# Moving half of the next pair's token transposes, and the work on them, ahead of the current pair's output products

## The chip, the cores and the metric

The kernel runs on one core of one Trainium2 chip. The metric is the device time of one execution in microseconds. TensorE multiplies matrices, VectorE and ScalarE do elementwise work, GpSimd small helper operations, and SyncE issues most DMAs. Each engine takes its own instructions in order; semaphores order them among each other.

## The reference

Input x has 8 chunks of 512 tokens of 512 features. In short:

```
xn = layernorm(x)
q, k, v = xn @ Wq.T + bq, xn @ Wk.T + bk, xn @ Wv.T + bv
context = phi(q) * cumsum(phi(k) * v, over tokens) * 32 ** -0.5     # phi(a) = elu(a) + 1
s = context @ Wo.T + bo
h = fwht(xn * SU_ug) ; up, gate = h @ W_up.T * .., h @ W_gate.T * ..   # 2048 hidden
z = fwht(silu(gate) * up * SU_dp) @ W_down.T * Wscale_dp
out = x + s * silu(z)
```

`fwht` is a Walsh-Hadamard transform, `phi(q)` and the cumulative sum are elementwise along the tokens. The kernel folds both transforms into the weights once.

## The kernel before

All matmuls are done on pairs of 16-bit parts: each operand is split into a high and a low half, and a product is three matmuls (high x high, high x low, low x high), of 128 x 128 by 128 x 512, accumulated in one PSUM bank. There are 8 banks of 128 x 512.

The eight chunks are worked in four pairs p = 0 to 3. Pair 0 also prepares the weights. In each of pairs 1 to 3, TensorE goes through 22 groups of seven products (a Strassen scheme: 7 products in place of 8, with sums of the tokens as operands), then through the "down" quads, four for each of the two chunks 2p and 2p+1 (`down_quad(c, a)`, 48 matmuls each), and after each chunk's quads through the output product of the attention (`out_product(c, t)`, four tiles t of 12 matmuls). Quads write the banks D_BANK = (7, 0, 1, 2), output products the banks R_BANK = (3, 4, 5, 6).

Between these stands the preparation of the next pair's tokens. The tokens x are loaded and normalised (`ln_stats`, `normalise_pair` on VectorE, the root on GpSimd). TensorE transposes them, in two halves kk = 0, 1, each 16 transposes of 128 x 128 (`transposes`), into the four banks R_BANK, the same that the output products use. Each half then goes through four steps:

- `x_high` (ScalarE): copies one bank aside (`b12`) and three as 16-bit high halves;
- `x_sums` (VectorE): seven operations of 128 x 512, sums for the scheme and low halves; the last one counts `x_read`;
- `t_high` (ScalarE): the high halves of the four sums, one operation of 128 x 2048;
- `t_low` (VectorE): their low halves, two operations of 128 x 1024; the last one counts `x_ready`.

The products of pair p+1 wait for `x_ready` of both halves.

On VectorE the order at the end of pair p is: the last additions of the products (`summed`), the maximum of the context, `ln_stats(p + 1)`, `normalise_pair(p + 1)` (counts `xn_ready`), the context's scale, eight `split_ctx`, `out_scale`, then `outputs(2p)`: for each tile the gate's argument from a D bank (`gate_argument`, counts `z_ready`), silu by ScalarE (`silu_outs`), the attention's part from an R bank (`gated`, counts `o_read`) and the residual. Then come `x_sums` and `t_low` of both halves, then `outputs(2p + 1)`. On TensorE the transposes of half 0 stand after quad 0 of chunk 2p+1, those of half 1 after its quad 2. `out_product(2p)` waits for the split context and its weights, and `out_product(2p + 1)` for `x_ready` of half 1. The diff shows the waits.

Lines to follow: transposes L1567, output product L1642, down quads L1608, products L1517; VectorE's normalisation L917, first context scale L857, splits L1049 and L1050, `out_scale` L1245, gate argument L1242, `gated` L1251, `x_sums` L942 to L951, `t_low` L960, additions L971; ScalarE's `x_high` L628 and L630, `t_high` L635. In pair 0, `first_transposes` is L1553, the first product group L1419, its token low halves L930, and a fold of weights L1452.

Of the kernel before, what the change touches and what calls it, by code (L numbers as in the profile page):

```python
# [26 lines left out]
PAIRS = CHUNKS // 2  # L27
# [82 lines left out]
def nth(p, g):  # L110

    return GROUPS * (p - 1) + g
# [42 lines left out]
def build(nc, x, wk_t, wv_t, wq_t, wo_t, ug_t, down_t, vecs, rows, ident_in, hada_in, out):  # L155
# [5 lines left out]
    with ExitStack() as ctx_stack:  # L161
# [98 lines left out]
        x_read, x_ready = sem("x_read"), sem("x_ready")  # L260
# [342 lines left out]
        def _(act):  # L603
# [13 lines left out]
            def x_high(p, kk):  # L617
                n = 2 * p + kk
                act.wait_ge(xp_done, 4 * n + 4)
                if not kk:  # L620
                    act.wait_ge(h_ready, 32 * p)
                    if p == 1:
                        act.wait_ge(plain_done, 4 * GROUPS)
                    else:
                        act.wait_ge(product_done, len(ORDER) * (p - 1))
                else:
                    act.wait_ge(t_made, 4 * (n - 2))
                act.activation(b12, bank[R_BANK[2]][:, :], ACT.Copy).then_inc(b12_copied, 1)  # L628
                for b, r in ((B11, 0), (B21, 1), (B22, 3)):
                    act.activation(xops[:, kk, HI, b, :], bank[R_BANK[r]][:, :], ACT.Copy).then_inc(x_hi, 1)  # L630

            def t_high(p, kk):
                n = 2 * p + kk
                act.wait_ge(t_made, 4 * (n - 2) + 4)
                act.activation(xops[:, kk, HI, T1:T4 + 1, :], t_sums, ACT.Copy).then_inc(x_hi, 1)  # L635
# [167 lines left out]
            def silu_outs(c):  # L803
                for t in range(TB):
                    act.wait_ge(z_ready, 4 * c + t + 1)
                    act.activation(gate_g[:, t % 2, :], gate_g[:, t % 2, :], ACT.Silu).then_inc(gate_ready, 1)  # L806
# [22 lines left out]
            for p in range(1, PAIRS):  # L829
                for g in range(GROUPS):  # L830
                    group(p, g)
                for j in (C22, C21, C12):
                    take(p, GROUPS - 1, j)
                silu_outs(2 * p)
                if p < PAIRS - 1:
                    x_high(p + 1, 0)
                    t_high(p + 1, 0)
                    x_high(p + 1, 1)
                    t_high(p + 1, 1)
                silu_outs(2 * p + 1)  # L840

        @block.vector
        def _(dve):
# [90 lines left out]
            def x_sums(p, kk):  # L934
                n = 2 * p + kk
                m = 4 * (n - 2)
                r = [bank[b][:, :] for b in R_BANK]
                dve.wait_ge(b12_copied, n - 1)
                dve.wait_ge(x_hi, 4 * n + 1)
                if kk:  # L940
                    dve.wait_ge(x_ready, n)
                dve.tensor_tensor(t_sums[:, 0, :], b12, r[0], ALU.subtract).then_inc(t_made, 1)  # L942
                dve.tensor_tensor(xops[:, kk, LO, B11, :], r[0], xops[:, kk, HI, B11, :], ALU.subtract)
                dve.wait_ge(x_hi, 4 * n + 3)
                dve.tensor_tensor(t_sums[:, 2, :], r[3], b12, ALU.subtract).then_inc(t_made, 1)
                dve.wait_ge(t_made, m + 1)
                dve.tensor_tensor(t_sums[:, 1, :], r[3], t_sums[:, 0, :], ALU.subtract).then_inc(t_made, 1)
                dve.tensor_tensor(xops[:, kk, LO, B21, :], r[1], xops[:, kk, HI, B21, :], ALU.subtract)
                dve.wait_ge(t_made, m + 3)
                dve.tensor_tensor(t_sums[:, 3, :], r[1], t_sums[:, 1, :], ALU.subtract).then_inc(t_made, 1)  # L950
                dve.tensor_tensor(xops[:, kk, LO, B22, :], r[3], xops[:, kk, HI, B22, :], ALU.subtract) \  # L951
                    .then_inc(x_read, 1)
# [92 lines left out]
            def split_ctx(p, n):  # L1045
                at = ctx_s(n)
                if n:
                    dve.wait_ge(ctx_split, 8 * p + n)
                prep.after(dve.tensor_scalar(at[:, HI, :], ctx_f(n), s_c[:, 0:1], None, ALU.mult))  # L1049
                dve.scalar_tensor_tensor(at[:, LO, :], ctx_f(n), s_c[:, 0:1], at[:, HI, :],  # L1050
                                         ALU.mult, ALU.subtract).then_inc(ctx_split, 1)
# [192 lines left out]
            def out_scale():  # L1244
                prep.after(dve.tensor_scalar(o_out[:, :], i_c[:, :], o_in[:, 0:1], None, ALU.mult))  # L1245
# [146 lines left out]
            for p in range(1, PAIRS):  # L1392
                for g in range(GROUPS):
                    group(p, g)
                last_sums(p)
                ctx_absmax(p)
                if p < PAIRS - 1:
                    ln_stats(p + 1)
                    normalise_pair(p + 1)
                ctx_scale(p)  # L1400
                for n in range(8):
                    split_ctx(p, n)
                out_scale()
                outputs(2 * p)
                if p < PAIRS - 1:
                    x_sums(p + 1, 0)
                    t_low(p + 1, 0)
                    x_sums(p + 1, 1)
                    t_low(p + 1, 1)
                outputs(2 * p + 1)  # L1410

        @block.tensor
        def _(pe):
# [142 lines left out]
                                mm.then_inc(xp_done, 1)  # L1556

            def transposes(p, kk):
                if kk:
                    pe.wait_ge(x_read, 2 * p - 1)  # L1560
                else:
                    pe.wait_ge(xn_ready, 8 * p + 8)
                for r, (c, k) in enumerate(((0, kk), (0, kk + 2), (1, kk), (1, kk + 2))):
                    if kk == 0:
                        pe.wait_ge(o_read, 8 * p - 8 + r + 1)
                    for t in range(TB):
                        mm = pe.transpose(bank[R_BANK[r]][:, t * P:(t + 1) * P],  # L1567
                                          x_ln[:, TB * c + t, k * P:(k + 1) * P], ident[:, :])
                    mm.then_inc(xp_done, 1)
# [44 lines left out]
            def down_quad(c, a):  # L1614
                for ts in ((0, 1), (2, 3)) if a == 0 else ((0, 1, 2, 3),):
                    down_part(c, a, ts)

            def out_product(c, t):
                p, cc = divmod(c, 2)
                n = GROUPS + (KB + 1) * cc + KB  # L1620
                slot = slot_of(p, n) if p else 0
                if t == 0:
                    pe.wait_ge(ctx_split, 8 * p + 8)
                    if p == 0:
                        pe.wait_ge(o_made, 1)
                    else:
                        pe.wait_ge(slot_loaded[slot], 16 * loads_into(p, n))
                    if p == 0 and cc == 0:
                        wait_taken(pe, 0, GROUPS - 1, PLAIN_BANKS.index(R_BANK[0]))
                        pe.wait_ge(stage_made, 4 * FP)  # L1630
                    elif cc == 0:
                        pe.wait_ge(summed, 3 * nth(p + 1, 0))
                    elif p < PAIRS - 1:
                        pe.wait_ge(x_ready, 2 * p + 4)
                if p == PAIRS - 1 and cc:
                    pe.wait_ge(o_read, 4 * c - 4 + t + 1)
                cols = slice(t * P, (t + 1) * P)
                n = 0
                for f in range(KB):
                    at = ctx_s(4 * (f % 2) + 2 * (f // 2) + cc)  # L1640
                    for s, ws in ((HI, HI), (HI, LO), (LO, HI)):
                        mm = pe.matmul(bank[R_BANK[t]][:, :], at[:, s, cols], o_weight(slot)[:, f, ws, :],  # L1642
                                       start=(n == 0), stop=(n == 3 * KB - 1))
                        n += 1
                mm.then_inc(o_done, 1)
# [3 lines left out]
            for p in range(PAIRS):  # L1649
                for g in range(GROUPS):  # L1650
                    if p == 0:
                        first_group(g)
                    else:
                        group(p, g)
                for a in range(KB):
                    if a or not p:
                        down_quad(2 * p, a)
                for t in range(TB):
                    out_product(2 * p, t)
                for a in range(KB):  # L1660
                    down_quad(2 * p + 1, a)
                    if a in (0, 2) and p < PAIRS - 1:
                        transposes(p + 1, a // 2)
                for t in range(TB):
                    out_product(2 * p + 1, t)

# [44 lines left out]
```

## Time and profile before

| | |
|---|---|
| median of 3 runs | 1337.85 us (1336.74 to 1338.49) |
| profiled execution, its own time | 1337.85 us |
| its span, first to last instruction | 1336.0 us |
| mean granted clock of TensorE | 0.998 of full speed |
| TensorE busy | 98% of the span |
| VectorE, ScalarE, GpSimd busy | 64%, 39%, 3% |

The profile's page gives busy times and the chain of work that ended last; the trace behind it gives every instruction with its start, its duration and what released it. Where a row has a bracket, this is the engine's idle time just before the row and what ended it. Rows without a bracket follow the one before without idle time worth naming. A matmul's record overlaps the next by up to 0.16 us, so differences of starts are used where pieces follow each other.

### The profile page before, as it was taken

To read this page: it belongs to the slowest core of one execution; us is meant where nothing else is said; L and a number is where in the kernel's file an instruction comes from. 1 tells how busy PE (TensorE), PEld (TensorE's weight loads), DVE (VectorE), ACT (ScalarE), POOL (GpSimd) and SP (SyncE) were. 2 spreads that over 40 slices of the span, in tenths; PEclk is the share of its full clock that TensorE was granted. 3 is DMA by queue.
4 is the path that set the end of the run, shared out by engine and by line. 5 is a ranking of instruction groups with operands and counts; after the bars stand their busy time and mean duration, and the time that the engine had idled before them with its cause. 6 is when DMAs were issued, how large, how long until landed. Compare 5 with 4: busy or idle time off the path is not lost.

```text
span 1336.0 us, 16024 instructions
## 1 busy us (share of the span) xinstructions
PE 1307.3 (98%) x6100; PEld 598.5 (45%) x6100; DVE 853.3 (64%) x1365; ACT 527.3 (39%) x815; POOL 41.8 (3%) x72
## 2 busy tenths in 40 slices
PE   5999999999999999999999999999999999999998
PEld 3434444444444444444454444444444444444443
DVE  6897999959446778655735765546735664555433
ACT  5844555540124655541014554442013654443000
POOL 0100100000000001000000000000000000000000
PEclk9999999999999999999999999999999999999999
DMA  9612555446255256435344233234344333333230
GB/s 370 249 75 106 188 200 205 176 179 218 81 214 185 97 201 222 158 127 187 107 148 157 99 123 126 97 124 170 114 157 135 132 112 126 105 117 116 105 126 32
DMA packets 47548, 199.38 MB, mean 149 GB/s; under 512 B 5104, under 2 KB 5360, under 8 KB 31984
## 3 DMA queue, kind: packets, MB, share of 16 engines
q1 hardware_dynamic: 41424, 176.87, 36.9%
q0 software_dynamic: 6048, 21.50, 4.3%
q8 instruction: 48, 0.79, 0.2%
q14 instruction: 28, 0.23, 0.1%
HBM read 153.26 MB, written 45.09 MB: 148 GB/s over the span
## 4 chain that ended last, share of the span: by engine, by line
PE 87%; DVE 5%; issue 3%; ACT 3%; DMA 2%; SPq 0%; DVEq 0%; ACTq 0%
PE bank L1517 37%; PE bank L1608 25%; PE bank L1419 15%; PE bank L1642 6%; PE bank L1452 2%; PE bank L1463 1%; ACT work L726 1%; DVE work L987 1%; ACT work L729 1%; PE bank L1567 1%; DVE work L977 1%; DVE work L971 1%; DMA h_all<-scr_f 1%; DMA work<-in_x 0%; DMA ring<-scr_d 0%
## 5 line engine op out<-in xcount | busy, mean ns | idle before, releaser
L1517 PE MATMUL bank<-xops,ring 128*128 128x512 f16 x2772 | 602.5, 379 | 3.9 <-DVE work L971 1.9
L1517 PEld LDWEIGHTS bank<-xops,ring 128*128 128x128 f16 x2772 | 269.6, 98 | 335.9 <-issue 7.0
L1608 PE MATMUL bank<-ring,h_all 128*128 128x512 f16 x1536 | 334.3, 379 | 0.2 <-DMA ring<-scr_d 0.2
L971 DVE TENSOR_TENSOR work<-bank,work 128x512 f32<-128x512 f32 x198 | 134.1, 686 | 181.9 <-PE bank L1517 167.9
L1419 PE MATMUL bank<-xops,ring 128*128 128x512 f16 x1056 | 238.5, 380 | 1.9 <-DVE xops L930 1.9
L1608 PEld LDWEIGHTS bank<-ring,h_all 128*128 128x128 f16 x1536 | 150.2, 98 | 180.4 <-DMA ring<-scr_d 0.7
L716 ACT ACTIVATE work<-bank 128x512 f32<-128x512 f32 x198 | 117.8, 595 | 245.1 <-PE bank L1517 245.1
L1419 PEld LDWEIGHTS bank<-xops,ring 128*128 128x128 f16 x1056 | 103.0, 98 | 142.0 <-issue 30.8
L806 ACT ACTIVATE gate_g<-gate_g 128x512 f32<-128x512 f32 x32 | 19.9, 630 | 229.5 <-DVE gate_g L1242 229.5
L746 ACT ACTIVATE h_all<-work 128x512 f16<-128x512 f32 x128 | 78.0, 624 | 73.3 <-DVE work L1010 73.2
L1019 DVE TENSOR_TENSOR h_all<-work,h_all 128x512 f16<-128x512 f32 x128 | 87.6, 686 | 8.0 <-ACT h_all L746 6.6
L1642 PE MATMUL bank<-ring,ctx 128*128 128x512 f16 x384 | 84.2, 379 | 0.0
L977 DVE SCALAR_TENSOR_TENSOR work<-work 128x512 f32<-128x512 f32 x64 | 44.2, 690 | 53.8 <-ACT work L729 53.6
L1242 DVE TENSOR_TENSOR gate_g<-bank,row 128x512 f32<-128x512 f32 x32 | 21.4, 689 | 69.7 <-PE bank L1608 69.1
L1010 DVE SCALAR_TENSOR_TENSOR work<-bank,up_out,work 128x512 f32<-128x512 f32 x56 | 41.8, 746 | 25.7 <-PE bank L1517 11.4
L1642 PEld LDWEIGHTS bank<-ring,ctx 128*128 128x128 f16 x384 | 37.6, 98 | 45.3
L739 ACT ACTIVATE work<-work,gate_out 128x512 f32<-128x512 f32 x72 | 51.1, 714 | 5.4 <-DVE work L971 5.0
L942 DVE TENSOR_TENSOR work<-work,bank 128x512 f32<-128x512 f32 x6 | 4.1, 688 | 75.6 <-ACT xops L630 75.6
L1010 DVE SCALAR_TENSOR_TENSOR work<-work,up_out 128x512 f32<-128x512 f32 x72 | 51.9, 744 | 0.3
L739 ACT ACTIVATE work<-bank,gate_out 128x512 f32<-128x512 f32 x56 | 38.0, 679 | 22.3 <-PE bank L1419 21.1
L992 DVE TENSOR_TENSOR_SCAN work<-work 128x512 f32<-128x512 f32 x32 | 39.2, 1224 | 1.1
L628 ACT ACTIVATE work<-bank 128x512 f32<-128x512 f32 x6 | 3.6, 597 | 90.2 <-PE bank L1567 90.2
(166 smaller groups left out, 877.9 us busy)
## 6 DMA issues: line engine op xcount, KB each, us to landing
ring<-scr_g SPq DMA_DIRECT2D x66, 1024.0 KB, 4.8
ring<-scr_d SPq DMA_DIRECT2D x32, 1024.0 KB, 4.8
scr_g<-ring SPq DMA_DIRECT2D x22, 512.0 KB, 3.3
h_all<-in_ug_t SPq DMA_DIRECT2D x8, 1024.0 KB, 14.4
x_res<-in_x SPq DMA_DIRECT2D x32, 256.0 KB, 3.4
out<-x_res SPq DMA_DIRECT2D x32, 256.0 KB, 6.8
scr_g<-ring POOLq DMA_DIRECT2D x14, 512.0 KB, 3.0
work<-in_x SPq DMA_DIRECT2D x6, 1024.0 KB, 6.5
```

Source lines behind the costliest of these rows:

```text
L716: act.activation(tile(g, j), chain_bank(g)[:, :], ACT.Copy).then_inc(copied, 1)
L739: act.activation(tile(g, j), src, ACT.Silu, scale=gate_out[:, at:at + 1]).then_inc(act_tiles, 1)
L746: act.activation(h[:, i, TILE_OF[j], HI, :], tile(g, j), ACT.Copy).then_inc(h_hi, 1)
L971: dve.tensor_tensor(tile(g, j), at[:, :], tile(g, j), ALU.add).then_inc(summed, 1)
L977: dve.scalar_tensor_tensor(tile(g, j), exp_tile(n), 1.0, tile(g, j), ALU.min, ALU.add) \
L992: dve.tensor_tensor_scan(tile(g, j), tile(g, j), tile(g, j), 0.0, ALU.add, ALU.bypass) \
L1010: dve.scalar_tensor_tensor(tile(g, j), src, up_out[:, at:at + 1], tile(g - 1, j), ALU.mult, ALU.mult).then_inc(h_made, 1)
L1019: dve.tensor_tensor(at[:, LO, :], tile(g, j), at[:, HI, :], ALU.subtract).then_inc(h_ready, 1)
L1419: mm = pe.matmul(plain_bank(g, j)[:, :], at[:, s, 2 * dh + kk, r, :], xops[:, kk, xs, PLAIN_B[dh][c], :], start=(n == 0), stop=(n == len(t ...
L1517: mm = pe.matmul(to[:, :], weight_of(slot, s, b, kk), xops[:, kk, xs, c, :], start=(a == 0 and m in (P1, P2, P5)), stop=(a == 5), skip_gro ...
L1608: mm = pe.matmul(bank[D_BANK[t]][:, :], at[:, s, cols], w[:, :, ws, :], start=(a == 0 and b == 0 and n == 0), stop=(a == KB - 1 and b == K ...
L1642: mm = pe.matmul(bank[R_BANK[t]][:, :], at[:, s, cols], o_weight(slot)[:, f, ws, :], start=(n == 0), stop=(n == 3 * KB - 1))
```

## The change

At the ends of pairs 1 and 2 half 0 of the next pair's tokens is taken earlier. TensorE issues its transposes between quads 2 and 3 of chunk 2p. VectorE does its `x_sums` and `t_low` before `out_scale` and `outputs(2p)`, and ScalarE its `x_high` and `t_high` before `silu_outs(2p)`. The transposes of half 1 move to after quad 0 of chunk 2p+1. The waits follow: half 0 waits for the last additions (`summed`) in place of `o_read`; half 1 waits for `o_read` of each tile and no longer for `x_read`; `out_product(2p)` waits for `x_ready` of half 0 (count 2p+3) in place of `summed`, and `out_product(2p + 1)` as before for that of half 1 (2p+4). At the end of pair 0 the order is as before, and in pair 3 there are no transposes.

```diff
--- before.py
+++ after.py
@@ -831,10 +831,11 @@
                     group(p, g)
                 for j in (C22, C21, C12):
                     take(p, GROUPS - 1, j)
-                silu_outs(2 * p)
                 if p < PAIRS - 1:
                     x_high(p + 1, 0)
                     t_high(p + 1, 0)
+                silu_outs(2 * p)
+                if p < PAIRS - 1:
                     x_high(p + 1, 1)
                     t_high(p + 1, 1)
                 silu_outs(2 * p + 1)
@@ -1400,11 +1401,12 @@
                 ctx_scale(p)
                 for n in range(8):
                     split_ctx(p, n)
+                if p < PAIRS - 1:
+                    x_sums(p + 1, 0)
+                    t_low(p + 1, 0)
                 out_scale()
                 outputs(2 * p)
                 if p < PAIRS - 1:
-                    x_sums(p + 1, 0)
-                    t_low(p + 1, 0)
                     x_sums(p + 1, 1)
                     t_low(p + 1, 1)
                 outputs(2 * p + 1)
@@ -1556,12 +1558,14 @@
                                 mm.then_inc(xp_done, 1)
 
             def transposes(p, kk):
-                if kk:
-                    pe.wait_ge(x_read, 2 * p - 1)
-                else:
+                if p == 1 and kk:
+                    pe.wait_ge(x_read, 1)
+                if kk == 0:
                     pe.wait_ge(xn_ready, 8 * p + 8)
+                    if p > 1:
+                        pe.wait_ge(summed, 3 * nth(p, 0))
                 for r, (c, k) in enumerate(((0, kk), (0, kk + 2), (1, kk), (1, kk + 2))):
-                    if kk == 0:
+                    if kk == (p > 1):
                         pe.wait_ge(o_read, 8 * p - 8 + r + 1)
                     for t in range(TB):
                         mm = pe.transpose(bank[R_BANK[r]][:, t * P:(t + 1) * P],
@@ -1628,10 +1632,12 @@
                     if p == 0 and cc == 0:
                         wait_taken(pe, 0, GROUPS - 1, PLAIN_BANKS.index(R_BANK[0]))
                         pe.wait_ge(stage_made, 4 * FP)
+                    elif p == 0:
+                        pe.wait_ge(x_ready, 4)
+                    elif p < PAIRS - 1:
+                        pe.wait_ge(x_ready, 2 * p + 3 + cc)
                     elif cc == 0:
-                        pe.wait_ge(summed, 3 * nth(p + 1, 0))
-                    elif p < PAIRS - 1:
-                        pe.wait_ge(x_ready, 2 * p + 4)
+                        pe.wait_ge(summed, 3 * nth(PAIRS, 0))
                 if p == PAIRS - 1 and cc:
                     pe.wait_ge(o_read, 4 * c - 4 + t + 1)
                 cols = slice(t * P, (t + 1) * P)
@@ -1655,12 +1661,16 @@
                 for a in range(KB):
                     if a or not p:
                         down_quad(2 * p, a)
+                    if a == 2 and 0 < p < PAIRS - 1:
+                        transposes(p + 1, 0)
                 for t in range(TB):
                     out_product(2 * p, t)
                 for a in range(KB):
                     down_quad(2 * p + 1, a)
-                    if a in (0, 2) and p < PAIRS - 1:
-                        transposes(p + 1, a // 2)
+                    if a == 0 and p < PAIRS - 1:
+                        transposes(p + 1, 1 if p else 0)
+                    if a == 2 and p == 0:
+                        transposes(1, 1)
                 for t in range(TB):
                     out_product(2 * p + 1, t)
```

## Rows read from the trace of the kernel before

**Rows 1.** The page's first part: busy us of each engine, share, instructions.
```profile
PE 1307.3 (98%) x6100; PEld 598.5 (45%) x6100; DVE 853.3 (64%) x1365; ACT 527.3 (39%) x815; POOL 41.8 (3%) x72
```

**Rows 2.** TensorE's waits: us in total, times, longest.
```profile
PE bank L1553 <- DVE work L917: 14.5, 1, 14.5
PE bank L1452 <- DVE h_all L1160: 2.5, 1, 2.5
PE bank L1517 <- DVE work L971: 1.9, 6, 0.3
```

**Rows 3.** TensorE in order of time: start us, us, engine, line, tiles.
```profile
615.00 36.42 PE L1608 MATMUL bank<-ring,h_all 128*128 128x512 f16 x168
651.26 10.52 PE L1642 MATMUL bank<-ring,ctx 128*128 128x512 f16 x48
...
671.98 1.91 PE L1567 MATMUL bank<-ident,work 128*128 128x128 f32 x16
673.72 20.88 PE L1608 MATMUL bank<-ring,h_all 128*128 128x512 f16 x96
694.44 1.91 PE L1567 MATMUL bank<-ident,work 128*128 128x128 f32 x16
...
730.25 10.65 PE L1517 MATMUL bank<-xops,ring 128*128 128x512 f16 x48 [0.23 <-ACT work L716]
...
959.99 10.52 PE L1642 MATMUL bank<-ring,ctx 128*128 128x512 f16 x48
```

**Rows 4.** VectorE in order of time, end of pair 1.
```profile
633.81 0.17 DVE L914 TENSOR_SCALAR rstd<-rstd 128x8 f32<-128x8 f32 x1 [4.14 <-POOL rstd L538]
634.02 3.74 DVE L917 TENSOR_SCALAR work<-work,mean_var,rstd 128x512 f32<-128x512 f32 x8
637.68 0.14 DVE L857 TENSOR_SCALAR pw<-ctx_max_all 128x1 f32<-128x1 f32 x1
...
648.78 0.21 DVE L1245 TENSOR_SCALAR o_out<-i_c,o_in 128x1 f32<-128x1 f32 x1
651.53 1.29 DVE L1242 TENSOR_TENSOR gate_g<-bank,row 128x512 f32<-128x512 f32 x2 [2.54 <-PE bank L1608]
...
662.07 0.74 DVE L1251 SCALAR_TENSOR_TENSOR s_f<-bank,o_out,row 128x512 f32<-128x512 f32 x1
```

**Rows 5.** VectorE in order of time, `x_sums` and `t_low` of half 0.
```profile
675.11 0.69 DVE L942 TENSOR_TENSOR work<-work,bank 128x512 f32<-128x512 f32 x1 [10.85 <-ACT xops L630]
...
680.84 2.36 DVE L960 TENSOR_TENSOR xops<-work,xops 128x1024 f16<-128x1024 f32 x2 [1.45 <-ACT xops L635]
```

**Rows 6.** ScalarE in order of time, the same half.
```profile
673.92 0.60 ACT L628 ACTIVATE work<-bank 128x512 f32<-128x512 f32 x1 [14.42 <-PE bank L1567]
...
678.82 1.91 ACT L635 ACTIVATE xops<-work 128x2048 f16<-128x2048 f32 x1 [2.84 <-DVE work L950]
```

**Rows 7.** VectorE in order of time, end of pair 2.
```profile
936.39 2.47 DVE L891 BATCH_NORM_STATS2 stats<-work 128x6 f32<-128x512 f32 x4 [1.55 <-DMA work<-in_x]
...
946.83 0.15 DVE L857 TENSOR_SCALAR pw<-ctx_max_all 128x1 f32<-128x1 f32 x1
...
957.92 0.21 DVE L1245 TENSOR_SCALAR o_out<-i_c,o_in 128x1 f32<-128x1 f32 x1
```

**Rows 8.** The chain that ended last, ahead of the first product.
```profile
19.87 2.40 DVE xops L930 x4
```

**Rows 9.** Stretches: length, busy us of each engine, TensorE's granted clock, DMA.
```profile
22.40:30.40 8.00, 8.00 (x46) 3.75 (x46) 5.21 (x16) 7.91 (x8) 0.70 (x2) 1.00 1.00 401
68.00:73.20 5.20, 2.78 (x13) 1.07 (x11) 5.17 (x6) 1.45 (x2) 0.00 (x0) 1.00 0.38 152
73.20:82.00 8.80, 8.74 (x29) 3.52 (x30) 8.05 (x28) 3.36 (x5) 0.68 (x2) 0.81 0.08 30
```

**Rows 10.** TensorE in order of time, the two early waits.
```profile
22.40 7.93 PE L1419 MATMUL bank<-xops,ring 128*128 128x512 f16 x36 [1.89 <-DVE xops L930]
...
73.26 1.51 PE L1452 MATMUL bank<-h_all,hada 128*128 128x512 f32 x2 [2.48 <-DVE h_all L1160]
```

## The prediction

> **What bounds the kernel now.** I read the page first. TensorE is busy 1307.3 of the 1336.0 us, the next engine (VectorE) 853.3 [rows 1]. So about 28.7 us of the span are all that any reordering could win, and every microsecond in which TensorE is made to wait is added to the time. The reader is to see there that nothing but TensorE's own stream sets the end.
>
> Next, who ends TensorE's waits [rows 2]. The largest are 14.5 us at the start and one of 2.5 at 70.8 us; the other seven lines have under 2 us each, the sums (L971) with six waits of up to 0.3 first among them. No line of the view names the transposes of the pair loop (L1567) or the output product (L1642). So the wait on `x_read` or on `o_read` before the transposes, and the wait on `x_ready` before the output product, which the change moves, cost nothing today.
>
> Then TensorE in order of time around the end of pair 1 [rows 3]. From 615.00 on each piece starts where the one before it ends, with no idle time named: 168 matmuls of down quads until 651.26 (3.5 quads in 36.26 us, so 10.36 each), there the output product of chunk 2 (as long as a quad, 48 matmuls), quad 0 of chunk 3, transposes from 671.98, two quads, transposes from 694.44, quad, output product, next pair. The first small wait comes only within the next pair's products, 0.23 us at 730.25; with four like it up to 783.86 they make 1.25 us.
>
> Last, VectorE and ScalarE over the same stretch [rows 4, 5, 6], because the change puts its work between the rows of these two. VectorE is the engine to look at: after the statistics of the layernorm it waits 4.14 us for GpSimd's root, then come eight normalisations, the scale of the context and its eight splits, back to back until 648.78. It idles only 2.5 us before the outputs of chunk 2, and then 10.85 us before `x_sums`.
>
> **The change part by part.** The first pair's boundary (pair 0 to 1) keeps its order: with p = 0 the transposes stand after quads 0 and 2 of chunk 1 as now, and the waits are the same numbers. The last pair has no transposes. What changes lies at the ends of pairs 1 and 2, so every term counts twice.
>
> *Work added or removed: none.* The 16 transposes of a half, 1.74 us (they start at 671.98 and the next quads at 673.72 [rows 3]), are issued once as before. The number of copies, sums and DMAs is the same. TensorE's busy time should stay.
>
> *Transposes of half 0, moved from after quad 0 of chunk 2p+1 to between quads 2 and 3 of chunk 2p.* The output product now starts at 651.26; quad 3 takes 10.36 before it; so quad 2 ends at 640.90. That is where the transposes go. They need `xn_ready`, the last normalisation: the eight L917 start at 634.02 and the next operation starts at 637.68 [rows 4], so they have 3.2 us to spare. In pair 2 the output product starts at 959.99 [rows 3], so quad 2 ends at 959.99 - 10.36 = 949.63 and the normalisations at 946.83 [rows 7]: 2.8 us to spare. Their wait on `summed` is for the pair's last addition, which stands ahead of all these on VectorE and so is long past. Cost: nothing now; it would cost what the loading of x is later than these 3 us. They no longer wait for `o_read`. Quad 3 then runs from 642.64 to 653.00, where the output product could start.
>
> *The new wait.* The output product of chunk 2p writes the banks that the transposes filled, so it must now wait until `x_sums` and `t_low` of half 0 have read them (`x_ready` 2p+3). How long does that take? Today, with VectorE free: transposes issued at 671.98, ScalarE's first copy at 673.92, `x_sums` from 675.11, ScalarE's wide copy 678.82 to 680.73, `t_low` from 680.84 to 683.20 [rows 5, 6]. From transposes to `x_ready` 11.22 us, of which VectorE's part, from its first subtraction, is 683.20 - 675.11 = 8.09 us.
>
> From 640.90 this would be done at 652.12, 0.9 us before the product: it would just fit, if VectorE were free at 644.03. It is not. VectorE works in order, and `x_sums` stands behind the eight splits of the context, which last until 648.78 (there `out_scale` starts today [rows 4]). So: 648.78 + 8.09 = 656.87, plus 0.13 from the end of the releasing VectorE group to the first matmul that it releases (a group of 2.40 us from 19.87, so 22.27 [rows 8], and 22.40 [rows 10]) = 657.00. TensorE could have started at 653.00. **Stall in pair 1: 4.00 us.**
>
> Pair 2 by the same rows: VectorE is free at 957.92 [rows 7], 0.4 us later in relation to TensorE because the second load of x landed later (1.55 us of idle at 936.39). 957.92 + 8.09 + 0.13 = 966.14 against 959.99 + 1.74 = 961.73. **Stall in pair 2: 4.41 us.** Together 8.41.
>
> The bounds of this term. Below: were ScalarE's copies done before, `x_sums` might run a little closer packed than 0.60 us each, but these rows already run back to back; I allow 0.3 us a pair. Above: the landing of x moves the end of the splits, by 0.4 us from one pair to the other; I allow 0.6 us a pair.
>
> *What is queued behind the wait.* On TensorE all the rest of the kernel. On VectorE, after `t_low`, come `out_scale` (0.21) and `outputs(2p)`. The quads of chunk 2p are by then done, so the first two gate arguments run at once, about 0.3 to 1.6 us after the output product's start. Today they run from 0.27 to 1.56 after it [rows 4]. So the output stage stands to the output product as today, its first tile waits 2.8 us for the product as today, and the banks that quad 0 of chunk 2p+1 wants are free as early. ScalarE's silus come after `t_high`, which is done 2.6 us before the product starts (5.62 us after `x_sums` begins [rows 5, 6]): no cost.
>
> *Transposes of half 1, moved from after quad 2 to after quad 0 of chunk 2p+1.* They wait for `o_read` of all four tiles. The last L1251 starts 10.8 us after the output product [rows 4] and the transposes 20.7 us after: 9 us to spare. Then 11.22 us to `x_ready`, against 1.74 + 31.08 (three quads) until the output product of chunk 2p+1 that now waits for it: 21 us to spare, where today there are 694.44 + 11.22 = 705.66 against 694.44 + 1.74 + 10.36 = 706.54, only 0.9. This slack is what the change gains, but it is slack at a place where TensorE did not wait. VectorE is idle there and the outputs of chunk 2p+1 stay as they are, so the next pair starts as now. DMAs are issued in the same order, each waits for TensorE or VectorE, and so moves along.
>
> *TensorE's clock.* A stall may cost more than its length. Where TensorE waited 2.48 us, until 73.26 [rows 10], the granted clock had been 1.00 and was 0.81 in the 8.8 us after it [rows 9]: of its two levels, 1.2 GHz for part of that stretch and 2.4 for the rest. That is 0.19 x 8.8 = 1.67 us lost. After the wait of 1.89 us before 22.40 the clock stayed 1.00 [rows 9, 10]. Ends: nothing (as after 1.89) and twice 1.67 (the stalls are 1.6 and 1.8 times as long as the one of 2.48). I take 1.67 each, because both stalls are nearer to, and longer than, the idle that lost it. Together 3.34.
>
> A page bears on this. The Trainium skill, "TensorE: Matmul & The Clock Gate", section "Why this matters for your kernels", advises to leave no idle gap of more than about 3 us between bursts of matmuls, since the clock falls back to half. Here the trace differs in size, since 2.48 us were enough; by the page as by the row both stalls would lose the clock, and with the clock kept, which the page would expect only of shorter stalls, the sum would be 3.34 us lower.
>
> **The sum.** The profiled execution took 1337.85 us for a span of 1336.0, so 1.85 lie outside it; it is also the median of the runs (1336.74 to 1338.49), so one sum serves for both. 1336.0 + 4.00 + 4.41 + 3.34 = 1347.75 of span, + 1.85 = **1349.6 us**, 0.9% slower.
>
> **The rivals.**
>
> 1. *The clock holds.* Stalls as worked out, no loss after them: 1337.85 + 8.41 = 1346.3; if one of the two loses it, 1347.9. For it: the gap of 1.89 us. Against: that of 2.48.
>
> 2. *The clock loses more.* Twice 1.67 after each stall: 1337.85 + 8.41 + 6.68 = 1352.9. For it: longer idle than any in the trace but the first; against: no row shows it.
>
> 3. *Not slower: the product does not wait.* This needs VectorE to be through `t_low` by 652.87, so `x_sums` to start by 644.8, 4.0 us before the splits end. That point decides. It could be only if the context were split or the normalisation done sooner, such as by GpSimd's root coming at once (VectorE waits 4.14 us for it in pair 1). Nothing in the change touches that chain. It would give 1337.9. If besides that the smoother boundary took away all the small waits of the next pairs, 2 x 1.25 us, 1335.3: even this is only 0.19%.
>
> 4. *The transposes wait as well.* If x lands over 3 us later, they stall TensorE before quad 3. But that wait mostly replaces the later one, as VectorE is late by the same amount: each further microsecond of lateness costs one, and no more. With 2 us in each pair 1353.6.
>
> **How the numbers follow.** Forecast (both or most of the clock loss) 0.70; the clock holds at one or both stalls 0.14; it loses more 0.07; transposes wait 0.02; no wait 0.05, of which nearly all is within the bound; something that makes it faster 0.02. I call 0.2% (2.7 us) about what a measurement of this kernel can tell from no change. Slower: 0.70 + 0.14 + 0.07 + 0.02 = 0.93; same 0.05; faster 0.02. The range: from the clock holding less 0.6 us for the packing and 0.4 for the run, 1345.3, to the clock losing twice, 1353.0. It leaves out "no wait" and the worst of rival 4.
>
> **What the profile after would show.** In the waits of TensorE a new line: the output product waiting for `t_low` on VectorE, twice, 4.0 and 4.4 us. In TensorE's timeline 16 transposes between quads 2 and 3 of chunks 2 and 4, with no idle before them. In VectorE's timeline `x_sums` directly behind the splits, with no idle before it, and no idle before the gate arguments. The granted clock at some 0.8 in the 9 us after each stall, and the output product taking some 12 us for 10.5. TensorE's busy time some 3.3 us higher by the slower clock alone. The second half's `x_ready` some 21 us ahead of its use. I am wrong if the context's splits end sooner in relation to TensorE, or if `x_sums` to `t_low` takes clearly less than 8.09 us.

## The result

The changed kernel took 1348.88 us (median of 4 runs, 1347.22 to 1349.52) against 1337.33 us for the kernel before in the same rounds (1336.74 to 1338.49). The ratio is 1.0084, with a 95% interval from 1.0065 to 1.0101: slower by 0.8%, or 11.55 us; 11.75 were forecast. The profiled execution took 1349.76 us, its span is 1347.9 us, 11.9 more than the span before. It is the longest of the changed kernel's five executions, so what its trace adds up to lies a little above the median.

First the waits of TensorE in the changed kernel (us in total, times, longest), which answer to [rows 2]:

```profile
PE bank L1555 <- DVE work L918: 14.6, 1, 14.6
PE bank L1648 <- DVE xops L961: 7.5, 2, 3.8
```

The second line is new. L1648 is the output product, L961 is `t_low`: twice the product waited for VectorE's last low half, 7.5 us together, and nothing like it stood in the kernel before.

TensorE in order of time at the ends of pair 1 and pair 2, against [rows 3]:

```profile
614.60 26.06 PE L1612 MATMUL bank<-ring,h_all 128*128 128x512 f16 x120
640.50 1.91 PE L1571 MATMUL bank<-ident,work 128*128 128x128 f32 x16
642.25 10.52 PE L1612 MATMUL bank<-ring,h_all 128*128 128x512 f16 x48
656.45 13.23 PE L1648 MATMUL bank<-ring,ctx 128*128 128x512 f16 x48 [3.68 <-DVE xops L961]
669.52 10.52 PE L1612 MATMUL bank<-ring,h_all 128*128 128x512 f16 x48
679.88 1.91 PE L1571 MATMUL bank<-ident,work 128*128 128x128 f32 x16
...
955.83 1.91 PE L1571 MATMUL bank<-ident,work 128*128 128x128 f32 x16
957.58 10.52 PE L1612 MATMUL bank<-ring,h_all 128*128 128x512 f16 x48
971.90 12.21 PE L1648 MATMUL bank<-ring,ctx 128*128 128x512 f16 x48 [3.79 <-DVE xops L961]
983.94 10.52 PE L1612 MATMUL bank<-ring,h_all 128*128 128x512 f16 x48
```

The transposes have no idle time before them, in either pair. The only gap is ahead of the output product. By starts it is 656.45 - (642.25 + 10.36) = 3.84 us in pair 1 (a quad takes 10.36 us by starts) and 971.90 - (957.58 + 10.36) = 3.96 in pair 2. Then the product itself is slow: from its start to the next quad's it is 669.52 - 656.45 = 13.07 us in pair 1 and 12.04 in pair 2, where 10.36 was usual. That is 2.71 and 1.68 us more for the same 48 matmuls.

So the sum is 3.84 + 3.96 of stall and 2.71 + 1.68 of slower product, 12.19. The changed kernel reached the half quad 0.40 us earlier (614.60, [rows 3] 615.00), which the change has no part in, and 0.1 is scattered: 11.9. This 0.40 is what is left of two larger differences that have nothing to do with the change. In the kernel before the clock was lost at 73.26 [rows 9, 10], in this execution it was not (1.00 there), and pair 1 began 1.9 us earlier; then TensorE waited 1.12 us at 505.17 and 0.43 at 523.89 for VectorE, of which the kernel before had 0.16. Single executions of one kernel differ by such amounts: the 27 of the kernel before below span 1335.57 to 1338.66 us.

VectorE over the same stretch, against [rows 4, 5]: the last split, then at once `x_sums`, `t_low`, `out_scale`, gate arguments.

```profile
633.25 0.17 DVE L915 TENSOR_SCALAR rstd<-rstd 128x8 f32<-128x8 f32 x1 [3.87 <-POOL rstd L538]
...
647.55 0.75 DVE L1051 SCALAR_TENSOR_TENSOR ctx<-ctx,s_c 128x512 f16<-128x512 f32 x1
648.22 0.68 DVE L943 TENSOR_TENSOR work<-work,bank 128x512 f32<-128x512 f32 x1
...
653.95 2.36 DVE L961 TENSOR_TENSOR xops<-work,xops 128x1024 f16<-128x1024 f32 x2 [1.45 <-ACT xops L635]
656.22 0.21 DVE L1246 TENSOR_SCALAR o_out<-i_c,o_in 128x1 f32<-128x1 f32 x1
656.47 1.29 DVE L1243 TENSOR_TENSOR gate_g<-bank,row 128x512 f32<-128x512 f32 x2
661.77 0.75 DVE L1252 SCALAR_TENSOR_TENSOR s_f<-bank,o_out,row 128x512 f32<-128x512 f32 x1 [4.01 <-PE bank L1648]
```

The reader sees the queue: the banks were filled at 642.3, but VectorE begins to read them at 648.22, when the eighth split is through, and ends at 656.31, 8.09 us later; 0.14 us after that the product starts.

And TensorE's granted clock (length, busy us and count, clock, DMA), in the gap and in the product of either pair:

```profile
652.70:656.40 3.70, 0.07 (x1) 0.83 0.65 230
656.40:669.50 13.10, 13.05 (x48) 0.79 0.04 17
968.00:971.80 3.80, 0.10 (x1) 1.00 0.65 231
971.80:983.90 12.10, 12.00 (x48) 0.86 0.03 14
```

The same view in short stretches shows when the clock changed:

```profile
655.20:655.40 0.20, 0.00 (x0) 0.50 0.97 410
662.00:662.50 0.50, 0.50 (x4) 1.00 0.00 0
972.00:972.30 0.30, 0.30 (x2) 1.00 0.53 219
972.60:973.00 0.40, 0.40 (x3) 0.50 0.00 0
976.00:976.50 0.50, 0.50 (x4) 1.00 0.00 0
```

In pair 1 the clock fell from 2.4 to 1.2 GHz at about 655.1, already within the gap, and rose at 662.0: 5.5 us of the product ran at half clock. In pair 2 it fell only at 972.6, 0.7 us after the product had begun, and rose at 976.0: 3.4 us at half clock. Half of each is what was lost, 2.8 and 1.7 us. By the long stretches 0.21 x 13.1 = 2.75 and 0.14 x 12.1 = 1.69 us: the slow products are explained by the clock alone. TensorE had been busy without a break before both gaps.

### The profile page after: what moved, and what is told of

Same layout as the page of the kernel before. It is cut to its first block, busy times and chain, and to the rows that moved or that the text cites. A ratio compares the mean times of both kernels' runs of the same rounds, so it can differ in the third digit from the quotient of the medians.

```text
span 1347.9 us, 16024 instructions
## 1 busy us (share of the span) xinstructions
PE 1311.1 (97%) x6100; PEld 599.5 (44%) x6100; DVE 853.2 (63%) x1365; ACT 528.6 (39%) x815; POOL 46.6 (3%) x72
## 4 chain that ended last, share of the span: by engine, by line
PE 77%; DVE 9%; ACT 4%; DMA 4%; issue 4%; SPq 0%; POOL 0%; DVEq 0%; ACTq 0%
PE bank L1519 35%; PE bank L1612 19%; PE bank L1421 13%; PE bank L1648 6%; PE bank L1454 2%; DMA h_all<-scr_f 2%; DMA work<-in_x 2%; ACT work L726 1%; ACT work L729 1%; PE bank L1465 1%; DVE work L988 1%; DVE ctx L1051 1%; DVE work L972 1%; DVE work L978 1%; DVE work L918 1%
## 5 line engine op out<-in xcount | busy, mean ns | idle before, releaser
L1648 PE MATMUL bank<-ring,ctx 128*128 128x512 f16 x384 | 88.6, 393 | 7.5 <-DVE xops L961 7.5
L1648 PEld LDWEIGHTS bank<-ring,ctx 128*128 128x128 f16 x384 | 38.5, 101 | 56.6 <-issue 14.2
L1252 DVE SCALAR_TENSOR_TENSOR s_f<-bank,o_out,row 128x512 f32<-128x512 f32 x32 | 23.9, 748 | 18.1 <-PE bank L1648 18.1
```

## The experiments

Theory: the whole loss is VectorE's lateness at the output product, plus what the clock loses after the gap. Rivals: TensorE's new order costs by itself (transposes and copies beside quad 3, or another wait that the first hides), and the slack won for half 1 is worth something which the stall covers up. Both idles filled, root's idle filled, stall in two gaps and eight cheap low halves ran together beside the kernel before (1336.99 us, 27 runs); three cheap low halves, transposes after quad 1, slack alone and the kernel before with cheap low halves ran together beside it too (1337.62 us, 19 runs). The changed kernel was not run again in these rounds. An estimate in the table is the kernel before in the same rounds plus the stalls and the product's excess, read by starts from the kernel's own trace as above. Stalls and clock losses are those of the one profiled execution; the median is over all. All times are in us.

| kernel | stalls, pair 1 and 2 | lost by the clock | estimate | measured median | ratio to before, 95% |
|---|---|---|---|---|---|
| changed kernel | 3.84, 3.96 | 2.71, 1.68 | 1349.5 | 1348.88 | 1.0065 to 1.0101 |
| both idles filled | 0, 0 | 0, 0 | 1337.0 | 1336.92 | 0.9993 to 1.001 |
| root's idle filled | 0, 0.86 | 0, 0 | 1337.9 | 1338.38 | 1.0001 to 1.0019 |
| stall in two gaps | 1.59 + 2.31, 1.99 + 2.31 | 0, 1.69 | 1346.9 | 1346.98 | 1.0065 to 1.0093 |
| eight cheap low halves | 0.73, 1.60 | 0, 0 | 1339.3 | 1338.93 | 1.001 to 1.0028 |
| three cheap low halves | 2.86, 3.05 | 0, 1.69 | 1345.2 | 1345.1 | 1.0045 to 1.0079 |
| transposes after quad 1 | 7.46, 7.20 | 2.61, 2.07 | 1357.0 | 1356.91 | 1.0131 to 1.0161 |
| slack alone | none | none | 1337.6 | 1337.97 | 0.9996 to 1.0015 |
| before, cheap low halves | none | none | 1337.6 | 1337.92 | 0.9992 to 1.0011 |

**Both idles filled.** In the changed kernel VectorE does part of the splits while it would wait for x and for GpSimd's root. TensorE's instructions stay. `ln_stats` calls `early` ahead of its wait for the second chunk of x, between the statistics of the two chunks; `...` stands for lines left out of a cut here and below.

```diff
-            def ln_stats(p):
+            def ln_stats(p, between=None):
...
+                        if t and between is not None:
+                            between()
                         dve.wait_ge(x_ln_loaded[t // TB], 16 * p)
...
+                def early():
+                    ctx_scale(p)
+                    split_ctx(p, 0)
+
                 if p < PAIRS - 1:
-                    ln_stats(p + 1)
+                    ln_stats(p + 1, early)
+                    for n in range(1, 4):
+                        split_ctx(p, n)
                     normalise_pair(p + 1)
-                ctx_scale(p)
-                for n in range(8):
+                else:
+                    ctx_scale(p)
+                for n in range(4 if p < PAIRS - 1 else 0, 8):
                     split_ctx(p, n)
```

> The changed kernel with VectorE's order inside its own idle times changed: the scale of the context and split 0 go between the statistics of the two chunks (where it waits for x), splits 1 to 3 between the statistics and the normalisation (where it waits for GpSimd's root); splits 4 to 7 stay. TensorE's order is that of the changed kernel. My theory (the whole loss is VectorE's lateness at the output product, and the clock after it): VectorE idles 0.61 + 3.87 us there in pair 1 and 1.53 + 2.84 in pair 2, the stalls are 3.84 and 3.95, so both go, and the clock stays: 1337.3 us (1336.5 to 1338.5), the time of the kernel before. Rival (the order of TensorE's own work, or transposes and copies beside quad 3, cost the time): at least 1345. Rival (slack at half 1 is worth something once the stall is gone): below 1336.

It took 1336.92 us, the ratio is 1.0001 (0.9993 to 1.001). Its VectorE and its TensorE in order of time at the end of pair 1:

```profile
632.80 0.17 DVE L917 TENSOR_SCALAR rstd<-rstd 128x8 f32<-128x8 f32 x1
...
642.06 0.69 DVE L945 TENSOR_TENSOR work<-work,bank 128x512 f32<-128x512 f32 x1 [0.20 <-ACT xops L630]
...
647.78 2.36 DVE L963 TENSOR_TENSOR xops<-work,xops 128x1024 f16<-128x1024 f32 x2 [1.45 <-ACT xops L635]
```

```profile
638.92 1.91 PE L1580 MATMUL bank<-ident,work 128*128 128x128 f32 x16
640.67 10.52 PE L1621 MATMUL bank<-ring,h_all 128*128 128x512 f16 x48
651.03 10.52 PE L1657 MATMUL bank<-ring,ctx 128*128 128x512 f16 x48
```

VectorE no longer waits for the root. It is ready before ScalarE's copies (it waits 0.20 us for them), `t_low` ends at 650.14 and the product starts at 651.03 with no wait, 0.9 us later: the margin that the prediction gave for a free VectorE. The whole loss is gone with TensorE's order left as changed, so this order costs nothing of itself. It is not faster than the kernel before either, so nothing was hidden under the stall.

**Root's idle filled.** The same with only the scale and splits 0 to 2, between the statistics and the normalisation.

```diff
                     ln_stats(p + 1)
+                    ctx_scale(p)
+                    for n in range(3):
+                        split_ctx(p, n)
                     normalise_pair(p + 1)
-                ctx_scale(p)
-                for n in range(8):
+                else:
+                    ctx_scale(p)
+                for n in range(3 if p < PAIRS - 1 else 0, 8):
                     split_ctx(p, n)
```

> Only the wait for GpSimd's root is filled, with the scale and splits 0 to 2. My theory: VectorE is free 3.87 us earlier in pair 1 and 2.84 in pair 2, so stalls of about 0.1 and 1.1 us stay, too short to lose the clock: 1338.5 us (1337.5 to 1339.5). Rival (TensorE's order): at least 1345.

1338.38 us. In pair 1 the wait is gone, in pair 2 there is 0.86 by starts, since there part of VectorE's idle is the wait for x. The row, of TensorE in order of time:

```profile
961.74 10.52 PE L1652 MATMUL bank<-ring,ctx 128*128 128x512 f16 x48 [0.69 <-DVE xops L961]
```

The product after it took its usual length. The expected time, 1338.5 us, was right to 0.1 us; the stalls came out 0.1 and 0.2 us shorter than expected.

**Stall in two gaps.** One wait more on TensorE, within quad 3.

```diff
                     i, r = k % 8, k // 8
+                    if cc == 0 and 0 < p < PAIRS - 1 and a == 3 and b == 2:
+                        pe.wait_ge(t_made, 8 * p + 1)
```

> The changed kernel with one more wait on TensorE: in the middle of quad 3 of chunk 2p it waits for the first sum of x_sums. VectorE's times don't move, so in each pair the same 3.8 to 4.0 us of stall is only cut into two gaps, about 1.5 us in the quad and 2.3 before the output product. If the loss of the clock hangs on the length of one gap: no or less loss, at least 2.5 us below the changed kernel, 1344.5 to 1346.5. If it hangs on the idle time together, or on nothing of the gap: 1348 to 1350 as the changed kernel.

1346.98 us, between the two forecasts, and the time alone decides nothing. TensorE in order of time does:

```profile
648.49 5.35 PE L1614 MATMUL bank<-ring,h_all 128*128 128x512 f16 x24 [1.43 <-DVE work L943]
655.98 10.52 PE L1650 MATMUL bank<-ring,ctx 128*128 128x512 f16 x48 [2.14 <-DVE xops L961]
...
961.53 5.35 PE L1614 MATMUL bank<-ring,h_all 128*128 128x512 f16 x24 [1.83 <-DVE work L943]
969.02 12.21 PE L1650 MATMUL bank<-ring,ctx 128*128 128x512 f16 x48 [2.13 <-DVE xops L961]
```

The stall is about as long as before (3.90 and 4.30 us in all, by starts, against 3.84 and 3.96). With gaps of 1.43 and 2.14 the clock stayed, with 1.83 and 2.13 the product took 12.05 us: it was lost. So in this execution the clock cost 1.69 us in place of 4.39, but a gap of 2.13 us with another shortly before it can still lose the clock; that the loss hangs on the length of a single gap is not borne out. Nor do the times show that cutting the gap helps: the ratios to the kernel before, 1.0065 to 1.0093 here and 1.0065 to 1.0101 for the changed kernel, overlap, and the profiled execution had a higher mean clock (0.999) than the other three (0.996 to 0.997), so that the estimate meets the median is in part luck.

**Eight and three cheap low halves.** In pairs 1 and 2 the low half of the first eight, or first three, context splits is filled with zeros; the low-order part of the context is left out there. The kernel with three has `n < 3` in place of `n < 8`.

```diff
+                if 0 < p < PAIRS - 1 and n < 8:
+                    dve.memset(at[:, LO, :], 0.0).then_inc(ctx_split, 1)
+                    return
                 dve.scalar_tensor_tensor(at[:, LO, :], ctx_f(n), s_c[:, 0:1], at[:, HI, :],
```

> The changed kernel, where in pairs 1 and 2 the low half of each of the eight context splits is filled with zeros in place of being computed (this leaves out the low-order part of the context). The operation of 0.75 us becomes one that I expect between 0.14 and 0.49 us, so VectorE is free 2.1 to 4.9 us earlier. My theory: the stall shrinks by just that, to 0 to 1.8 us in each pair, and with it the clock's loss: 1337.3 to 1341. Rival (TensorE's order): 1345 or more.

> The changed kernel with only the first three low halves of each of pairs 1 and 2 filled with zeros. VectorE is free 0.8 to 1.8 us earlier. My theory: the stalls fall by exactly that, to 2.0 to 3.1 us; the clock is lost or kept by the length of the gap, so 1341.5 to 1347. It tells whether the stall follows VectorE one to one, and what a gap of such length does to the clock.

1338.93 and 1345.1 us. The filling takes 0.27 us in place of 0.75. VectorE of the kernel with eight:

```profile
643.27 0.27 DVE L1052 MEMSET ctx<- 128x256 uint32 x1
643.46 0.63 DVE L943 TENSOR_TENSOR work<-work,bank 128x512 f32<-128x512 f32 x1
```

and TensorE of it:

```profile
640.54 10.52 PE L1615 MATMUL bank<-ring,h_all 128*128 128x512 f16 x48
651.63 10.52 PE L1651 MATMUL bank<-ring,ctx 128*128 128x512 f16 x48 [0.56 <-DVE xops L961]
```

In pair 1 `x_sums` began 4.39 us before the product could have started in the changed kernel (648.22 against 652.61), 7.44 us before with eight cheap halves (643.46 against 650.90): 3.05 earlier, and the stall is 0.73 in place of 3.84, 3.11 less. With three, 0.98 earlier, stall 2.86, 0.98 less. In pair 2 eight cheap halves brought only 2.29 us (`x_sums` at 953.80, the product possible at 960.36), in part because VectorE waited 4.17 us for GpSimd's root there in place of 2.84; the stall fell by 2.36, to 1.60. The stall follows VectorE one to one, to within 0.1 us. The two products of the kernel with three, its TensorE:

```profile
654.37 10.52 PE L1651 MATMUL bank<-ring,ctx 128*128 128x512 f16 x48 [2.69 <-DVE xops L961]
...
966.14 12.21 PE L1651 MATMUL bank<-ring,ctx 128*128 128x512 f16 x48 [2.89 <-DVE xops L961]
```

An idle time of 2.69 us kept the clock, one of 2.89 lost it. Of the four executions of this kernel the profiled one was the fastest (1343.92 us against up to 1346.92) and had the highest mean clock (0.999 against 0.996 to 0.998), so the others probably lost more.

**The same in the kernel before**, as a control.

> The kernel before with the same edit as cheap_low_halves: the low halves of the context splits of pairs 1 and 2 are zeros. VectorE has 2.5 us of idle after the splits there, so its lateness costs nothing and saving it wins nothing: 1337.3 us, within 0.1%. If this kernel got faster by as much as the changed one does, the splits would be on the path in both, and my reading of the new wait would be wrong.

1337.92 us, ratio 1.0001 (0.9992 to 1.0011). The splits were off the path before and were put on it by the change.

**Transposes after quad 1.** The changed kernel with half 0 moved one quad further ahead.

```diff
-                    if a == 2 and 0 < p < PAIRS - 1:
+                    if a == 1 and 0 < p < PAIRS - 1:
                         transposes(p + 1, 0)
```

> The changed kernel with the transposes of half 0 one quad earlier still, after quad 1 of chunk 2p. My theory: they wait for the last normalisation, from 630.1 to about 637.2 in pair 1, 7.1 us, and the later wait vanishes, as quads 2 and 3 (20.7 us) cover the rest of VectorE's work: one wait replaces the other, 3.2 us longer in each pair, so 1355.3, and up to 2 us more or less by the clock. Rival (the two waits add up): 1362 or more.

1356.91 us. TensorE in order of time:

```profile
637.31 3.67 PE L1571 MATMUL bank<-ident,work 128*128 128x128 f32 x16 [7.30 <-DVE work L918]
640.77 21.77 PE L1612 MATMUL bank<-ring,h_all 128*128 128x512 f16 x96
662.38 10.52 PE L1648 MATMUL bank<-ring,ctx 128*128 128x512 f16 x48
```

Now the transposes wait for the last normalisation, and the product, at 662.38, does not wait: the second wait is replaced, not added to. The transposes took 3.46 us by starts in place of 1.74, and the two quads 21.61 in place of 20.72: the clock again, granted 0.71 over the 9.0 us from 637.30 on.

**Slack alone.** The kernel before, with only half 1 moved earlier.

```diff
-                    if a in (0, 2) and p < PAIRS - 1:
-                        transposes(p + 1, a // 2)
+                    if a == 0 and p < PAIRS - 1:
+                        transposes(p + 1, 0)
+                    if a == (1 if p else 2) and p < PAIRS - 1:
+                        transposes(p + 1, 1)
```

> The kernel before with one part of the gain alone: in pairs 1 and 2 the transposes of half 1 stand after quad 1 of chunk 2p+1, not after quad 2, and nothing else moves. x_ready of half 1 then comes 10 us ahead of the output product in place of 0.9. My theory: TensorE did not wait there, so nothing: 1337.3 us, within 0.1%. Rival (the narrow slack of 0.9 us costs something in executions that the trace does not show): up to 1 us faster.

1337.97 us, ratio 1.0006 (0.9996 to 1.0015): no gain. The slack was 0.9 us and is now 11.3 (`t_low` of half 1 ends at 694.87, the product starts at 706.13); TensorE never waited there.

## Why the prediction was right

*The new wait.* Right in place, releaser and size. 4.00 and 4.41 us were forecast, 3.84 and 3.96 came. The term `x_sums` to `t_low` was 8.09 us as read, and the release 0.14 in place of 0.13. What was off is when VectorE was free: 4.39 and 4.27 us before the product's possible start, in place of 4.22 and 3.81. It waits for GpSimd's root a little less in this execution, 3.87 us in place of the 4.14 of [rows 4] in pair 1, and 2.84 in place of 3.21 in pair 2. The cheap halves and the filled idles show that this time sets the stall, one to one.

*The clock.* Right in kind, 1.67 us for each stall; pair 2 lost 1.68, but pair 1 2.71. The single figure was the wrong form of this term: it took the loss from one gap [rows 9, 10], and at that very place gaps of the same 2.48 us cost nothing in two later kernels, while those of 3.79 and 3.68 us here cost 1.68 and 2.71. That the forecast hit so closely is in part luck: the two errors go against each other, 7.80 of stall in place of 8.41, 4.39 of clock in place of 3.34, so the sum came out only 0.4 below that of the profiled execution.

*Transposes of half 0 without a wait, and of half 1 too.* Right; neither row has idle time. The slack of half 1 is 21.6 us in pair 1, as forecast (its `t_low` ends at 691.09, the product starts at 712.71). That an earlier place would make them wait for the normalisation, and that such a wait mostly replaces the later one (rival 4), is shown by the kernel with the transposes after quad 1.

*Outputs and the next pair as before.* Right. The first `gated` came 5.3 us after the product's start in pair 1 in place of 2.8, as the product's first 5.5 us ran at 1.2 GHz, and still nothing waited for it: the next quad starts with no idle time. Behind the two boundaries TensorE waits only in the products, as before.

*The slack gains nothing.* Right, by the slack-alone kernel, and by the filled idles, which keep the slack for half 1 and tie with the kernel before.

*Rival 3, not slower.* I named its point: `x_sums` 4.0 us earlier, and the wait for GpSimd's root as the place where they lie. It did not come by itself, since nothing in the change touches that order; but done by hand it holds.

The runs show no version of this change that is faster than the kernel before: with all of the loss taken away the two are equal.

## What to carry to other kernels

A wait that costs nothing today has a margin, and a move spends it. Before a piece is moved ahead on the engine that sets the time, look up in the trace when the engine that must serve it is free, not how long its work takes: here the chain of 11.22 us would have fitted by 0.9 us, and the queue in front of it made it 4 us late. If such a move is wanted all the same, fill the serving engine's own waits with work that is already in its queue. And count a stall of TensorE as its length and an uncertain sum for the clock, here nothing to 2.7 us.

## What the runs showed of the hardware

The clock after a gap is less regular than its length suggests. Idle times as the rows name them, and what the work after them lost, each from one execution:

| idle before | lost after it |
|---|---|
| 0.56, 0.69, 1.44 us | nothing |
| 1.43 then 2.14 us | nothing |
| 1.83 then 2.13 us | 1.69 |
| 2.69 us | nothing |
| 2.48 us (kernel before, until 73.26) | 1.67 |
| 2.89 us | 1.69 |
| 3.79 us | 1.68 |
| 3.68 us | 2.71 |
| 7.05, 7.30 us | 2.07, 2.61 |

At the same place early in the program an idle time of 2.48 us kept the clock at 1.00 in the kernel with three cheap halves and with the transposes after quad 1, and one of 2.21 us lost it in the slack-alone kernel (0.80 over the 8.7 us from 73.30 on), where one of 2.20 kept it with both idles filled. So between 2.1 and 2.9 us either can happen, and in all five longer gaps the clock was lost, with 1.7 to 2.7 us. Why pair 1 lost a whole microsecond more than pair 2, with shorter idle, shows in the rows only so far: its clock fell 1.3 us before the gap was over and stayed down for 6.9 us, of which 5.5 fell on work, while in pair 2 it fell 0.7 us into the work and stayed down for 3.4. What decides when it falls and rises stays open.
